# Decoder layer on Trainium2: tanh in place of the sigmoid for the time scales, and a reordered start

## The reference

```
x = x + self_attention(layernorm(x))      # queries and keys through a 3-tap convolution, see below
x = x + cross_attention(layernorm(x), ctx, mask)
x = x + mixture(layernorm(x))             # 64 experts, 8 taken per token, and a shared one
```

```
q_in = x @ Wq.T + bq;  Q3 = conv1d(q_in, convq_w, convq_b);  Q = [q_in, Q3] @ qproj_w.T + qproj_b
k_in = x @ Wk.T + bk;  K3 = conv1d(k_in, convk_w, convk_b);  K = [k_in, K3] @ kproj_w.T + kproj_b
tau   = sigmoid(tau2 * gelu(depthwise_conv3(x, tau1)))
delta = sigmoid(del2 * gelu(depthwise_conv3(x, del1)))
scores = (Q @ K.T / sqrt(8)) * tau + delta;  out = softmax(scores) @ V
```

## Time and profile before

| | |
|---|---|
| median of three runs | 305.3 us |
| the profiled execution | 305.65 us |
| its span (first to last instruction) | 303.8 us |
| mean granted clock of TensorE | 0.987 |
| TensorE matmul busy | 288.5 us (95%) |
| VectorE busy | 227.5 us (75%) |
| ScalarE busy | 192.7 us (63%) |
| GpSimd busy | 185.1 us (61%) |

### The profile page before, as it was taken

How to read it: one execution, slowest core, us unless ns; L and a number is a source line. 1 busy time by engine, 2 the same in 40 slices (tenths; PEclk the granted TensorE clock), 3 DMA queues, 4 the chain that set the end, 5 groups by cost and what they waited for, 6 DMA issues and landing times.

```text
span 303.8 us, 5436 instructions
## 1 busy us (share of the span) xinstructions
PE 288.5 (95%) x1721; PEld 206.5 (68%) x1721; DVE 227.5 (75%) x511; ACT 192.7 (63%) x353; POOL 185.1 (61%) x258
## 2 busy tenths in 40 slices
PE   8999599999999999899879999999999999999995
PEld 3754476667655665466664788888888888888883
DVE  3695599789959886989796559788965766676664
ACT  2787647887784667466752797666655555555553
POOL 8430044087807880876167699999975666666661
PEclk9999789999999999999999999999999999999999
DMA  7703635447477233250000637866444344343321
GB/s 269 230 2 48 204 77 135 109 109 258 110 192 145 62 94 107 62 152 16 0 2 18 185 118 200 216 191 200 122 108 138 112 168 123 128 137 128 118 69 35
DMA packets 30636, 37.18 MB, mean 122 GB/s; under 512 B 5136, under 2 KB 19856, under 8 KB 30608
## 3 DMA queue, kind: packets, MB, share of 16 engines
q1 hardware_dynamic: 30608, 36.84, 43.3%
HBM read 28.43 MB, written 3.93 MB: 107 GB/s over the span
## 4 chain that ended last, share of the span: by engine, by line
PE 79%; DVE 14%; ACT 4%; issue 2%; ACTq 0%; DVEq 0%
PE bank L484 54%; PE bank L863 5%; PE bank L865 5%; PE bank L864 5%; PE bank L669 2%; DVE rawmax L1282 2%; PE bank L644 2%; PE bank L687 2%; DVE conv L1221 2%; DVE conv L1219 2%; PE bank L656 1%; PE bank L692 1%; PE bank L653 1%; PE bank L490 1%; DVE tauT L1349 1%
## 5 line engine op out<-in xcount | busy, mean ns | idle before, releaser
L1846 POOL TENSOR_TENSOR qbd<-vs,qbd 128x512 fp32r<-128x512 f32 x65 | 83.6, 1289 | 33.3 <-ACT qbd L1160 33.2
L484 PE MATMUL bank<-khl,stacks 128*128 128x512 f32 x396 | 101.5, 392 | 1.9 <-DVE vs L1643 1.9
L484 PEld LDWEIGHTS bank<-khl,stacks 128*128 128x128 f32 x396 | 73.5, 188 | 18.7 <-issue 3.7
L1674 DVE TENSOR_TENSOR conv<-bank,conv 128x512 f32<-128x512 f32 x60 | 41.5, 691 | 31.5 <-ACT bank L1124 28.3
L1124 ACT ACTIVATE bank<-bank 128x512 f32<-128x512 f32 x61 | 35.5, 582 | 44.0 <-PE bank L484 44.0
L1282 DVE TENSOR_REDUCE rawmax<-bank 128x4 f32<-128x512 f32 x64 | 43.2, 683 | 8.8 <-PE bank L484 7.8
L484 PE MATMUL bank<-stacks 128*128 128x512 f32 x96 | 42.8, 498 | 4.4 <-DVE stacks L1258 3.3
L1160 ACT ACTIVATE qbd<-vs 128x512 fp32r<-128x512 f32 x65 | 40.6, 625 | 7.1 <-DVE vs L1651 4.6
L1682 DVE TENSOR_TENSOR vs<-conv,bank 128x512 f32<-128x512 f32 x61 | 41.9, 687 | 2.1
L1048 ACT ACTIVATE conv<-bank 128x512 f32<-128x512 f32 x64 | 35.1, 596 | 6.3 <-PE bank L484 5.4
L1810 POOL TENSOR_TENSOR stacks<-ring,stacks 128x384 fp32r<-128x384 f32 x33 | 33.6, 1017 | 1.4
(11 more groups left out here) (238 smaller groups left out, 439.6 us busy)
## 6 DMA issues: line engine op xcount, KB each, us to landing
conv<-coefficient_rows SPq DMA_DIRECT2D x122, 128.0 KB, 2.9
ring<-w SPq DMA_DIRECT2D x33, 192.0 KB, 3.6
stacks<-stacks SPq DMA_DIRECT2D x68, 64.0 KB, 2.1
split_rows<-stacks SPq DMA_DIRECT2D x6, 256.0 KB, 2.6
stacks<-split_rows SPq DMA_DIRECT2D x16, 96.0 KB
split_rows<-khl SPq DMA_DIRECT2D x3, 512.0 KB, 4.3
stacks<-split_rows SPq DMA_DIRECT2D x8, 192.0 KB
pa<-pack_a SPq DMA_DIRECT2D x1, 706.0 KB, 5.4
```

Source lines behind the costliest of these rows:

```text
L484: return pe.matmul(out, lhsT, rhs, start=start, stop=stop)
L1674: dve.tensor_tensor(out, gate, spread[:, n % ROWS, :, :], ALU.mult).then_inc(gate_scaled, 1)
L1846: pool.tensor_tensor(hlo[:, n % 4, :].rearrange("p (b t) -> p b t", b=4), hx[n % 4], hhi[:, n % 4, :].bitcast(F32).rearrange("p (b t) -> p ...
```

## The change

- Tau's sigmoid becomes ScalarE's tanh of half the argument (with half the bias, `tau_half`, made once by GpSimd), and VectorE makes 0.5 * tanh + 0.5 of it in place, in a new instruction for each half.
- On TensorE `turn_inputs(0, 0)` goes ahead of the queries' `sum_bias`, and the keys' `sum_bias` behind the first query convolution.
- On ScalarE the second `copy_composed` and the copy of `tau2r` go behind first taps; the GELUs, fills and first taps are reordered; the keys' first high part goes ahead of the first tanh; the first tanh goes ahead of the last two GELUs.
- On VectorE the two additions of `foldb` go between the two groups of taps, and the keys' low parts are reordered: the first ahead of the scaled queries, the second ahead of the second low queries.

```diff
@@ tensor engine
             compose(0)
+            turn_inputs(0, 0, bank[0])
             sum_bias(0, "qp2T", "cqb", "bq")
-            turn_inputs(0, 0, bank[0])
             compose(1)
-            sum_bias(1, "kp2T", "ckb", "bk")
             turn_inputs(0, 1, bank[1])
...
                 convolve(0, convq, c, bank[5 + c]).then_inc(q_done, 1)
+                if c == 0:
+                    sum_bias(1, "kp2T", "ckb", "bk")
@@ scalar engine, order before
-            copy_composed(0, convq); copy_inputs(0, 0, 0); copy_composed(1, convk); copy_inputs(0, 1, 1)
-            tau2r copy
-            first_tap(0, 0); first_tap(0, 1)
-            fill_keys(1); fill_keys(2)
-            first_tap(1, 0)
-            early GELU 0; early GELU 1
-            first_tap(1, 1)
-            fill_keys(3)
-            late GELUs 0 (two halves); late GELUs 1 (two halves)
-            act.activation(half(tauT, c), four(3 + c), ACT.Sigmoid, bias=A("tau2b")).then_inc(tau_ready, 1)   # c = 0, 1
-            high_queries(0); high_queries(1)
-            act.wait_ge(k_done, 1)
-            high_keys(0, 0, 7, foldb[:, 1:2])
@@ scalar engine, order after
+            copy_composed(0, convq); copy_inputs(0, 0, 0); copy_inputs(0, 1, 1)
+            def time_scales(c):
+                act.wait_ge(tau_done, c + 1)
+                act.activation(half(tauT, c), four(3 + c), ACT.Tanh, scale=0.5, bias=tau_half[:, :]).then_inc(tau_ready, 1)
+            act.wait_ge(xT_copied, 2)
+            first_tap(0, 0, "tau1", "tau1b")
+            copy_composed(1, convk)
+            first_tap(0, 1, "tau1", "tau1b")
+            tau2r copy
+            first_tap(1, 0, "del1", "del1b")
+            early_gelu(0)
+            first_tap(1, 1, "del1", "del1b")
+            early_gelu(1)
+            fill_keys(1)
+            fill_keys(2)
+            late_gelu(0)
+            fill_keys(3)
+            act.wait_ge(bias_folded, 2)
+            act.wait_ge(k_done, 1)
+            high_keys(0, 0, 7, foldb[:, 1:2])
+            act.wait_ge(halves_ready, 2)
+            time_scales(0)
+            late_gelu(1)
+            time_scales(1)
+            high_queries(0)
+            high_queries(1)
             act.wait_ge(k_done, 2)
             high_keys(0, 1, 0, foldb[:, 1:2])
@@ vector engine
-            the two foldb additions, ahead of the taps
             later_taps(0, "tau1")
+            the two foldb additions
             later_taps(1, "del1")
...
+            low_keys(0, 0, 7, foldb[:, 1:2])
             for c in range(2):
                 dve.wait_ge(q_done, c + 1)
                 dve.wait_ge(tau_ready, c + 1)
+                dve.tensor_scalar(half(tauT, c), half(tauT, c), 0.5, 0.5, ALU.mult, ALU.add).then_inc(tau_scaled, 1)
+                dve.wait_ge(tau_scaled, c + 1)
                 dve.scalar_tensor_tensor(out=half(qc, c), in0=four(5 + c), scalar=foldb[:, 0:1], in1=half(tauT, c),
                                          op0=ALU.add, op1=ALU.mult).then_inc(q_ready, 1)
             low_queries(0, 0)
-            low_keys(0, 0, 7, foldb[:, 1:2])
+            low_keys(0, 1, 0, foldb[:, 1:2])
             low_queries(0, 1)
-            low_keys(0, 1, 0, foldb[:, 1:2])
@@ gpsimd
             pool.memset(halves[:, :], 0.5).then_inc(halves_ready, 1)
+            pool.wait_ge(ld_a, 16)
+            pool.tensor_scalar(tau_half[:, :], A("tau2b"), 0.5, None, ALU.mult).then_inc(halves_ready, 1)
             pool.wait_ge(xn_ready, B)
```

More of the change, by code:

```diff
@@ L101, in decoder_layer @@
         natural = qin[:, :, :].rearrange("p b t -> p (b t)")[:, 4 * P:6 * P].rearrange("p (n i) -> p n i", n=2)
-        negbias = sb("negbias", [P, 2])
+        small = sb("small", [P, 3])
+        negbias, tau_half = small[:, 0:2], small[:, 2:3]
         foldb = sb("foldb", [P, 2])
@@ L208, in decoder_layer @@
         tau_ready = sem("tau_ready")
+        tau_scaled = sem("tau_scaled")
         delta_done = sem("delta_done")
@@ L956, in _ @@
             copy_inputs(0, 0, 0)
-            copy_composed(1, convk)
             copy_inputs(0, 1, 1)
@@ L975, in _, with high_queries, late_gelu @@
             act.wait_ge(ld_a, 16)
[L976 to L988, removed]
-            fill_keys(3)
-            for r in range(2):
+            def high_queries(c):
+                act.wait_ge(q_ready, c + 1)
+                act.activation(half(qhl[:, 0, :, :], c), half(qc, c), ACT.Copy).then_inc(qhi_ready, 1)
+            def late_gelu(r):
                 act.wait_ge(conv_done, 3 + r)
@@ L993, in _, with early_gelu @@
                     act.activation(gelu_half(r, b), conv[:, 2 + r, b:b + 4, :], ACT.Gelu).then_inc(gelu_done, 1)
-            for c in range(2):
+            def early_gelu(r):
+                act.wait_ge(conv_done, r + 1)
+                act.activation(conv[:, r, :, :], conv[:, r, :, :], ACT.Gelu).then_inc(gelu_done, 1)
+            def time_scales(c):
                 act.wait_ge(tau_done, c + 1)
-                act.activation(half(tauT, c), four(3 + c), ACT.Sigmoid, bias=A("tau2b")).then_inc(tau_ready, 1)
-            def high_queries(c):
-                act.wait_ge(q_ready, c + 1)
-                act.activation(half(qhl[:, 0, :, :], c), half(qc, c), ACT.Copy).then_inc(qhi_ready, 1)
-            act.wait_ge(bias_folded, 2)
+                act.activation(half(tauT, c), four(3 + c), ACT.Tanh, scale=0.5, bias=tau_half[:, :]).then_inc(tau_ready, 1)
+            t0 = cols_a["tau2T"][0]
+            act.wait_ge(xT_copied, 2)
+            first_tap(0, 0, "tau1", "tau1b")
+            copy_composed(1, convk)
+            first_tap(0, 1, "tau1", "tau1b")
+            act.activation(tau2r[:, :, :, :].rearrange("p r h d -> p (r h) d"),
+                           pa[:, t0:t0 + 2 * H].unsqueeze(2).broadcast_to([P, 2 * H, DK]), ACT.Copy).then_inc(const_ready, 1)
+            first_tap(1, 0, "del1", "del1b")
[6 more added lines that the diff above has]
+            fill_keys(3)
+            act.wait_ge(bias_folded, 2)
+            act.wait_ge(k_done, 1)
[4 more added lines that the diff above has]
+            time_scales(1)
             high_queries(0)
             high_queries(1)
-            act.wait_ge(k_done, 1)
-            high_keys(0, 0, 7, foldb[:, 1:2])
             act.wait_ge(k_done, 2)
@@ L1209, in _ @@
             last.then_inc(picks_ready, 1)
-            dve.wait_ge(bias_summed, 2)
-            for n, bias in enumerate(("qpb", "kpb")):
-                dve.tensor_tensor(foldb[:, n:n + 1], bank[4][:, n:n + 1], A(bias), ALU.add).then_inc(bias_folded, 1)
             def later_taps(n, w):
@@ L1226, in _ @@
             later_taps(0, "tau1")
+            dve.wait_ge(bias_summed, 2)
+            for n, bias in enumerate(("qpb", "kpb")):
+                dve.tensor_tensor(foldb[:, n:n + 1], bank[4][:, n:n + 1], A(bias), ALU.add).then_inc(bias_folded, 1)
             later_taps(1, "del1")
@@ L1241, in values, with low_keys @@
                 last.then_inc(v_copied, 1)
+            def low_keys(n, c, b, bias):
+                dve.wait_ge(khi_ready, 2 * n + c + 1)
+                dve.scalar_tensor_tensor(out=half(khl[n][:, 1, :, :], c), in0=four(b), scalar=bias,
+                                         in1=half(khl[n][:, 0, :, :], c).bitcast(F32), op0=ALU.add,
+                                         op1=ALU.subtract).then_inc(klo_ready, 1)
+            low_keys(0, 0, 7, foldb[:, 1:2])
             for c in range(2):
```

## The result

The changed kernel took 303.68 us (median of 12 runs, 303.16 to 304.12), the kernel before 305.68 us in runs beside it. The ratio is 0.9943, interval 0.9926 to 0.996: faster, by 1.2 to 2.3 us. Forecast were 301.2 us and a range from 300.2 to 303.3, which the result misses. The profiled execution's span is 302.0 us against 303.8. Of the 29 executions of the kernel before that stood beside the first four experiments, six took 304.2 to 304.8 us at a mean granted clock of 0.993, and 23 took 305.5 to 307.0 at 0.983 to 0.989; its trace (305.65 us, 0.987) is of the second kind.

The account below looks back on a forecast made before the run. Late keys were taken to idle TensorE 3.26 us and slow its clock; 2.43 (start) + 1.5 (selection stage) + 0.1 (second slow stretch) gave about 4.05 us, so 301.2 us from a median of 305.3, range 300.2 to 303.3.

Parts of the forecast that it names:

- part on queues: SyncE's transfers: maxima rows issued to 31.8 us, split rows 31.85 to 34.9, step 1's key copies landing at 39.1.
- selections start: TensorE's first selection matmul: 31.15 us against 33.58, 2.43 us earlier, with no idle time in front.
- tanh needs no table load: ScalarE: tanh runs from GELU's loaded table; the rival that tables switch had chance 0.10 and 306.5 us.
- the taps stay in place: VectorE's convolution taps: -0.15 + 0.12 us is nothing, so the last tap result stays at 25.4 us.
- ScalarE's and VectorE's lines: Before the selections: ScalarE's second tanh ends at 27.5 us, gaining 1.7; VectorE's low second keys end at 30.8.
- The shift of TensorE's products: TensorE after the first convolution: everything shifts by +0.81 us because the bias sums move; context keys end at 31.13.
- the selection stage: Selection matmuls and evictions: 4.65 us against 6.18 at full clock, gain 1.5; rival of staying slow, chance 0.15.
- The gain at the first score: First score matmul: 2.43 us from the earlier start plus 1.5 from the selection stage, 3.95 us.
- the cover of 0.4 us: Step 1's key copies: landing at 39.1 us, wanted at 39.5, so 0.4 us of cover.
- the second slow stretch: Slow clock just after 43 us: nothing changes or about 0.5 us is won; taken as 0.1 us gain.
- transfers late: Rival, chance 0.07: split-row traffic in front of the key copies could cost 1.5 us, leaving gain 2.5, 302.8 us.
- the wait of 3.26 us: TensorE's idle time before the selections: late keys cost twice, as waiting and as a 0.50 clock after it.

Follow-up runs that it names:

- the first four experiments: Maxima rows spread on the changed kernel (305.39 us), spread on the kernel before (309.11), tanh alone on the kernel before (305.3), sigmoid between the GELUs in changed order (306.95).
- the spread run: Changed kernel with the eight maxima-row transfers moved from ahead of the split rows to behind the key copies of steps 1 to 7: 305.39 us, ratio 0.9988.
- order-only run: Changed kernel's order with the sigmoid instead of tanh, both sigmoids behind the last GELUs, no fix-up: 303.54 us, ratio 0.9935.
- the two kernels with the query rows behind: Changed kernel with the queries' three split-row transfers behind step 1's key copies (301.8 us), and the same with bias sums in old order on TensorE (301.91 us).
- the sums back: Changed kernel with the queries' split rows behind step 1's key copies and the bias sums in their old order on TensorE: 301.91 us, ratio 0.9881.
- the kernels at 301.8: Changed kernel with the queries' split rows behind step 1's key copies (301.8 us), the last key fill ahead of two GELUs (301.74), or both (301.82).

## Why the prediction was wrong

The step that failed is in its part on queues: "Four issues of 0.67 and 2.1 us to landing put them at 39.1 ... The cover is 0.4 us." It took the split rows' issue time from the kernel before (3.08 us), where the maxima rows had ended and the DMA engines stood nearly idle at 33 us (share 0.03). The same part had just moved the two towards each other, the maxima rows 1.4 us later and the split rows 1.7 us earlier. They met. The copies landed 2.4 us later than the 39.1 given: the split rows began 0.3 us late, took 1.5 us longer to issue and were followed by the key copies 0.1 us late, and three key copies took 2.54 instead of 2.01 us before the fourth was issued, which landed after 2.09 us as taken. The run with the last fill early and the one with the maxima rows on GpSimd show that an earlier start is enough to take the wait away or nearly so; the spread run, with no maxima rows in flight, has the 3.08 us back.

| step | forecast, us | measured, us |
|---|---|---|
| second tanh ends | 27.5 | 27.6 |
| fix-up at 512 columns | 0.39 | 0.43 |
| selections start | 31.15 | 31.10 |
| last eviction ends | 35.8 | 36.07 |
| first score matmul | 36.8 | 37.11 |
| split rows issued | 31.85 to 34.9 | 32.16 to 36.77 |
| key copies of step 1 landed | 39.1 | 41.50 |
| step 1's first score | 39.5 | 41.54 |

- Right: tanh needs no table load; the taps stay in place to 0.15 us, ScalarE's and VectorE's lines to 0.2 us, and the start. The shift of TensorE's products was 0.95 us (22.85 against 21.90) and not 0.81; the start agrees to 0.05 us because the selections began 0.17 us before the last product's end, so part of that closeness is luck.
- Right but 0.3 us large: the selection stage, 4.97 instead of 4.65 us; the clock stayed at 1.00 as taken. The gain at the first score is 3.68 us for 3.95.
- Wrong: the cover of 0.4 us. 2.4 us of lateness less the cover is the measured wait of 1.98 us.
- Wrong in sign: the second slow stretch, taken as +0.1 us. After the new idle time it was twice as long. The order-only run, with the clock at 1.00 all the way, goes from the same 41.53 us to the same block of 45 matmuls at 48.21 us, the changed kernel at 48.75: 0.54 us is what 6.8 us of slow clock cost there. A stretch of 3.4 us cost nothing: of the two kernels with the query rows behind, the one whose trace has it takes 6.85 us over this way and the one whose trace has none (the sums back) 6.84.
- The rival "transfers late" named the right wait, with a chance of 0.07 and at most 1.5 us, but not its cause: it charged the split rows' own traffic in front of the key copies. In the spread run that traffic (350 to 389 GB/s from 32 to 36 us) stood there and nothing was late; it took the maxima rows, and the queue's late start. The rival left 2.5 us of gain; 1.8 to 2.0 are left.
- Taken as certain: that the wait of 3.26 us brings the slow clock, which gave the stage's 1.5 us. The run with the spread maxima on the kernel before had the same wait and no slow clock behind it. The two kinds of execution of the kernel before lie 1.5 us apart or a little more (305.65 against about 304.2), which fits a first slow stretch that only some of them have; no trace of the faster kind was taken, so that is not shown. If it holds, against those executions (about 304.2 us) the changed kernel gains 0.5 us and the kernels at 301.8 gain 2.4, which is the earlier start alone. Both are estimates from the medians.
- With one fill or three transfers moved, the forecast gain is there: 301.74 and 301.8 us, ratio 0.987; forecast was 301.2 for a median of 305.3, which is 0.9866. The time in us still misses by 0.5, since the kernel before has a median of 306.0 beside these runs.

## What to carry to other kernels

When work on the path gets earlier by some microseconds, follow every in-order queue that must deliver beside it, with the time at which it can begin and not only what stands in it; the issue time read here while the DMA engines were idle did not hold once two groups of transfers met. A cover of 0.4 us is a rival of equal standing and not a term of zero. Before a fast step is bought (here tanh), look at whether the next thing waited for moves with it: the same change was worth nothing with one transfer order and 1.7 us with another. And where the kernel that is compared with has executions of two kinds, find out which kind the trace is of before the difference is put into a sum.

## What the runs showed of the hardware

- Tanh and GELU share a loaded table: the order tanh, GELU, GELU, tanh ran without a load, while sigmoid, GELU, GELU, sigmoid needed three of 1.28 us. Each of these began 0.02 us after the activation in front of it had ended, and the next one began 0.01 us after the load, so a switch cost 1.3 us here.
- A transfer's issue can hold SyncE's queue: split-row transfers of 256 KB took 0.33 to 0.65 us each before, and one took 1.89 us while the maxima rows still moved (70 to 82 GB/s from 30 to 33 us). With those issued by GpSimd instead, the six still took 4.59 us; with them away, 3.08.
- An idle TensorE is not always followed by the slow clock: after 3.26 us of idle time the granted clock was 0.50 in the kernel before and 1.00 in its twin with the maxima rows spread.
- Multiply-and-add of 128x512 float32 in place on VectorE took 0.43 us, inside the bounds of 0.26 and 0.52 worked out from the row at 256 columns.
